# A five-stage attention kernel: GpSimd's root goes ahead of its gathers, the next x is normalised two slots sooner, and the next projection weights are loaded ahead of the spread

## What is computed

```python
xn = layernorm(x) * g + b
q, k, v = xn @ wq, keys @ wk, keys @ wv        # keys: xn itself in stages 2 and 3, else the context
p = exp(scale * (q @ k.T) + mask)
o = (p @ v) / p.sum(-1)
x = x + o @ wo + bo
if stage in (0, 2, 4):
    x = x + gelu(layernorm(x) @ w1 + b1) @ w2 + b2
```

## Time and profile before

| | |
|---|---|
| median of the runs shown | 5038.94 us |
| the profiled execution, its own time | 5035.45 us |
| its span, first to last instruction | 5033.6 us |
| around the span | 1.85 us |
| TensorE (PE) busy | 4666.1 us, 93% of the span |
| VectorE (DVE) busy | 3036.8 us, 60% |
| ScalarE (ACT) busy | 2308.4 us, 46% |
| GpSimd (POOL) busy | 1068.9 us, 21% |
| DMA, mean | 40 GB/s |
| bodies 0 to 41 | from 0 to about 3790 us, the tail behind it |

### The profile page before, as it was taken

One profiled execution on the slowest core, in us unless ns is written; L12 is line 12 of the kernel. 1 busy time (PEld: TensorE's weight loads), 2 busy tenths in 40 slices (PEclk: granted clock), 3 DMA queues, 4 the chain that ended last, 5 costly groups with the idle time before them and its releaser, 6 DMA issues.

```text
span 5033.6 us, 66240 instructions
## 1 busy us (share of the span) xinstructions
PE 4666.1 (93%) x24484; PEld 1880.0 (37%) x24484; DVE 3036.8 (60%) x7970; ACT 2308.4 (46%) x3011; POOL 1068.9 (21%) x991
## 2 busy tenths in 40 slices
PE   6999999989998999999988889999989999999999
PEld 2333333433332333343444433333333333333333
DVE  6777776556767777665565565555534455545554
ACT  4454554456664444434445454444443333333332
POOL 0111211111111211111111111211113333333333
PEclk9999999999999999999999999999999999999999
DMA  1111111121121111001211121111120000000000
GB/s 60 35 51 52 48 41 44 35 87 56 58 66 51 37 37 33 30 31 42 73 61 56 57 71 42 52 37 35 39 77 21 13 1 13 13 13 13 1 13 9
DMA packets 164465, 201.67 MB, mean 40 GB/s; under 512 B 36273, under 2 KB 119601, under 8 KB 162866
## 3 DMA queue, kind: packets, MB, share of 16 engines
q1 hardware_dynamic: 141106, 176.34, 10.5%
q0 software_dynamic: 23040, 21.10, 1.7%
HBM read 128.86 MB, written 68.42 MB: 39 GB/s over the span
## 4 chain that ended last, share of the span: by engine, by line
PE 61%; issue 19%; DVE 14%; ACT 4%; POOL 1%; DMA 1%; DVEq 0%; SPq 0%; POOLq 0%; ACTq 0%
PE psO L721 8%; PE small L650 8%; PE psT L696 6%; PE small L657 5%; PE psT L926 5%; PE psS L678 4%; PE psT L779 3%; DVE nmb L1171 3%; PE psT L650 2%; PE psT L886 2%; PE psO L941 2%; PE psT L896 2%; PE psT L941 2%; PE psT L702 2%; DVE xn L1148 2%
## 5 line engine op out<-in xcount | busy, mean ns | idle before, releaser
L991 ACT ACTIVATE probs<-psT 128x1024 f32<-128x1024 f32 (+3 forms) x1280 | 1159.7, 960 | 1211.2 <-PE psT L696 1042.0
L1171 DVE TENSOR_REDUCE nmb<-psS 128x1 bf16<-128x512 f32 x1024 | 649.8, 685 | 293.4 <-PE psS L678 292.8
L1168 DVE CUSTOM_DVE_ANT_0 out<-psS,pens_sb 128x512 f32<-128x512 f32 x1024 | 665.4, 685 | 250.4 <-issue 248.7
L696 PE MATMUL psT<-low 32*128 32x512 f32 (+3 forms) x5120 | 755.0, 608 | 29.4 <-ACT probs L991 26.5
L721 PE MATMUL psO<-probs,V 128*32 128x512 f32 (+3 forms) x5120 | 670.5, 597 | 20.6 <-DVE probs L1180 19.0
L678 PE MATMUL psS<-out 32*128 32x512 bf16 (+3 forms) x2560 | 595.6, 380 | 97.1 <-DVE nmb L1168 46.4
L1354 DVE TENSOR_REDUCE parts<-psS 128x2 bf16<-128x1024 f32 x256 | 314.9, 1230 | 531.4 <-PE psS L913 531.4
L1097 ACT ACTIVATE probs<-psT 128x1024 f32<-128x1024 f32 x256 | 262.0, 1023 | 524.9 <-PE psT L929 524.9
L678 PEld LDWEIGHTS psS<-out 32*128 32x128 bf16 x2560 | 148.6, 91 | 796.9 <-issue 444.0
L779 PE MATMUL psT<-out,W 128*128 128x512 f32 x768 | 382.9, 620 | 0.4
L1021 ACT ACTIVATE low<-small,vec 128x256 f32<-128x256 f32 (+1 forms) x464 | 261.9, 617 | 232.8 <-PE small L650 232.7
(11 more groups left out here) (178 smaller groups left out, 5942.4 us busy)
## 6 DMA issues: line engine op xcount, KB each, us to landing
o_mid<-out SPq DMA_DIRECT2D x160, 256.0 KB, 2.0
oN<-o_mid POOLq DMA_DIRECT2D x160, 128.0 KB, 3.5
oN<-r_mid SPq DMA_DIRECT2D x80, 256.0 KB
x_mid<-xe SPq DMA_DIRECT2D x40, 512.0 KB, 2.9
xw<-x_mid SPq DMA_DIRECT2D x36, 512.0 KB, 4.1
xe<-x_mid SPq DMA_DIRECT2D x36, 512.0 KB, 5.0
cT<-ctxT SPq DMA_DIRECT2D x20, 512.0 KB, 5.5
W<-wm SPq DMA_DIRECT2D x6, 1024.0 KB, 8.5
```

Of the source, the lines that this page charges most:

```text
L696: last = nc.tensor.matmul(psT[j][:, q0:S], Kf[rows_of(j), q, a, c, kt * P:(kt + 1) * P], Qf[rows_of(j), q, a, c, q0:S], start=True, stop=p ...
L991: nc.scalar.activation(probs[:, i % 2, two, q0:S], psT_all[:, two, q0:S], ACT.Exp, scale=float(DH) ** -0.5)\
L1168: nc.vector.tensor_tensor_reduce(junk[:, e, 0:n], psS[e][:, 0:n], penalty, 1.0, -3.0e38, ALU.add, ALU.max, at).then_inc(sem[f"s_read{e}"], 1)
L1171: nc.vector.tensor_reduce(at, psS[e][:, 0:n], AX, ALU.max).then_inc(sem[f"s_read{e}"], 1)
```

## The change

It makes three edits.

1. GpSimd does `rsqrt(nxt, 1)` ahead of `gather_outputs(prev)`.
2. The statistics of the next x stand in slots 0 and 1 instead of 2 and 3. Its normalisation stands in slot 3 (first half) and slot 4 (second half) instead of all in slot 5.
3. On SP the wait for v3 and the load of the next stage's Wqkv come ahead of `spread_recips` also where `prev` is in an MLP stage (bodies 8 and 24). The load of the context keeps its place and its wait.

```diff
-X_STATS, X_NORMALISE = (2, 3), (5, 5)
+X_STATS, X_NORMALISE = (0, 1), (3, 4)
...
                 late = prev is not None and prev.s in MLP
+                if new_stage:
+                    wait_taken(sp, place, "cur", "v3")
+                    sp.dma_start(Wqkv[:], wa[nxt.s, :, 0:N_QKV]).then_inc(qkv_in, 16)
                 if late:
                     spread_recips(prev)
-                if cur is not None and (new_keys or new_stage):
-                    wait_taken(sp, place, "cur", "v3")
-                if new_stage:
-                    sp.dma_start(Wqkv[:], wa[nxt.s, :, 0:N_QKV]).then_inc(qkv_in, 16)
                 if new_keys:
+                    if cur is not None:
+                        wait_taken(sp, place, "cur", "v3")
                     sp.dma_start(cT[:], keys).then_inc(sem["ctx_in"], 16)
                 if prev is not None and not late:
                     spread_recips(prev)
...
             def body(place, prev, cur, nxt):
+                if nxt is not None:
+                    rsqrt(nxt, 1)
                 if prev is not None:
                     gather_outputs(place, prev)
-                if nxt is not None:
-                    rsqrt(nxt, 1)
                 if prev is not None:
                     pool.wait_ge(sem["xe_in"], count("xe_in", prev, 16))
```

## The result

The changed kernel took 5009.2 us (median of five runs, 5001.9 to 5022.6) against 5038.9 before: the ratio is 0.9947, 95% interval 0.9934 to 0.9959. So it is faster by 0.53%, about 27 us, where 66 were forecast. The execution that was profiled is the fastest of the five, 5001.92 us; against the profiled one of before (5035.45) it gains 33.5 us. The comparison of the two traces is of these two executions, so it shows somewhat more than the medians do: the profiled execution has a mean clock of 0.985, the other four 0.980 to 0.982.

A forecast was written before the change was run, and what follows sets the result against it. TensorE bounds the kernel, busy 93%, with 73.3 us of x0 waits and 121 us lost to its clock. Terms 29 + 29 + 0 + 1 + 0 + 0 + 7 = 66 us give 4969.5, median 4973; range 4925 to 5016.

The forecast's parts named there:

- rival C: x0's wait replaced by a new one as VectorE's reordered list delays maxima in step 1 or 3; 5013 us, chance 0.22.
- Reading of before: TensorE waits 73.3 us at x0 for VectorE's normalisation in bodies 2 to 39, and its clock falls behind those waits.
- Masked bodies: Twelve masked MLP bodies (2 to 7, 18 to 23): 19.5 us of waits and 10.5 of clock, less one; gain 29 us.
- Stage 3: Bodies 27 to 32: waits 19.6 us and clock 13.8, less 4.5 for VectorE's later maxima of step 3; gain 29 us.
- Stage 4: Bodies 34 to 39: the finished unit's way ends last, so TensorE stands at y instead of x0; gain about 0.
- Stage 1 with 10, 17 and 33: Bodies 10 to 17 and 33: 9 us of waits and 6 of slow stretches go, as much comes back; 0, bounds -10 and +12.
- Wqkv: Bodies 8 and 24: q projection stops waiting for its weights, while the spread takes some back; gain 7 us, bounds 0 and 12.
- Rival D: VectorE's normalisation holds up GpSimd's issue of the gathers, costing 12 us in bodies 9, 25, 34 to 39; 4985 us, chance 0.08.
- A: The forecast itself: x0's wait goes and y caps stage 4; 4973 us, own bounds 4945 to 5005, chance 0.52.
- B: Nothing caps: all 73 us of waits go, 50 us of slow stretches are recovered, y follows; 4911 us, chance 0.10.
- E: Root still late because the statistics wait for xw in slot 0, so the order changes nothing; 5039 us, chance 0.04.
- F: Statistics in slots 0 and 1 delay m1 and v2, so TensorE stands in step 1 of every body; 5087 us, chance 0.04.

## Why the prediction was right and wrong

The sign and the range (4925 to 5016) held, the 66 us did not: 27 by the ratio, 34 in the traces. That the range held is owed to rival C, for whose sake it reached so far up, and not to the forecast's own bounds (4945 to 5005).

- **Reading of before**: x0's wait and the clock behind it, right as far as they went. All 38 waits went. But I put the lateness of xn down to the root and the slot. The run with the add first in the old order shows that the add's place alone was worth 1.23%, some 60 us, and 45.8 of the 73.3 us of waits.
- **Masked bodies**, 29 forecast, 33.6 measured. Right: in body 4 the add had begun before the second pair and was past half, and the pair took 1.68 us.
- **Stage 3**, 29 forecast, 7.6 measured, 6.0 of these in body 32. The step that failed is "two tiles each, between maxima", costed at 0.75 us in step 3 of VectorE. It measured 3.16 us. I had written that the add runs beside the normalisation in stages 3 and 4 and makes it 3.00 us, and then took the clear duration for the moved halves: I moved the root past the gathers and wrote that the bias add queues behind them, but never asked where in VectorE's list it would then fall. With the add out of the way stage 3 gained 31.2, so the rest of the term stood.
- **Stage 4**, 0 forecast, 9.5 us lost. That the way of the finished unit ends last was right, and "nothing in this way starts sooner" too. But the held pair made it start later: the reciprocals stand 8.6 us into each of bodies 34 to 39 and not 5.3, and y waits 20.1 us. With the add first the reciprocals stand at 6.0 and the stage is 1.6 us below before.
- **Stage 1 with 10, 17 and 33**, 0 forecast with bounds -10 and +12, 7.5 lost: 5.6 in body 17 and 2.9 in body 10, while 33 gained 2.8. In body 10 it was the hold (one tile of the second pair took 2.60 us; with the add first the body falls from 74.1 to 69.2). In body 17 the hold is one of two things. The limit took 3.17 us beside the add and TensorE waited 2.20 us behind it; the three us from 1546 have a clock of 0.63. With the add first this wait is gone, but a wait for maxima 4.7 us into the body is followed by six us at half clock, and the body is 97.0 us for 97.8 (92.2 in before). Body 17 of the changed kernel, then of the kernel with the add first (the wait, and the window behind it):

```profile
1540.60 3.17 DVE L1181 TENSOR_TENSOR probs<-probs,parts 128x1024 f32<-128x1024 f32 x1
1544.45 0.39 PE L679 MATMUL psS<-out 32*128 32x512 bf16 x1 [2.20 <-DVE nmb L1169]
```

```profile
1522.92 0.39 PE L679 MATMUL psS<-out 32*128 32x512 bf16 x1 [1.50 <-DVE nmb L1169]
...
1524.00:1530.00 6.00, 6.00 (x23) 2.12 (x22) 4.41 (x16) 0.00 (x0) 2.52 (x4) 0.50 0.39 91
```

  Body 17 of the changed kernel has such an early wait too, 1.36 us at 3.5 us into the body, and before has none over 0.6 there. That is the "stall of 1.4 us in step 1" of the prediction.

- **Wqkv**, 7 forecast: 8.9 in bodies 8 and 24 of the changed kernel, part of it the x0 waits; 6.6 (one trace) in the run with this edit alone. Right.
- **Rival C** came nearest in time (5013 to 5009) and said where: a new wait in the same place. It was right for stage 3 and wrong for the masked bodies, and its cause, VectorE's reordered list, is not what the runs show, but for the early wait in body 17.
- **Rival D** had the right pair of engines and the wrong way round. Beside the normalisation the gathers' issue took 2.50 to 2.64 us, where it takes 2.50 alone, so 0.14 us at most; it is VectorE that is held, by the add. The Trainium skill's page "SBUF — State Buffer" (Who interferes with whom) has both directions: whichever of the two issues first keeps the port pair for its whole instruction, and a VectorE instruction with two SBUF inputs contends with a GpSimd instruction that reads SBUF, as does one in a 2-port mode. The trace agrees with that for the limit, in both directions: 3.24 us for 1.22 in the rows of the run with both halves in slot 3; and in body 4 of before, where a limit has its start 0.17 us ahead of the adds of the MLP bias, the limit took its 1.22 and the first add 1.64 us for 0.72. That the loser is out for one instruction of the other fits body 27 of before (0.82 us a tile) and not the changed kernel: there one tile lasted 2.43 us beside adds of 0.7 us each. I used the half of the rule that speaks of descriptors and not the half that priced the change.
- **A** (4973) and **B** (4911) lie on either side of what the kernel gives with the add first (4945), 28 and 34 us away; **E** and **F** did not come, but F's mechanism is what the second edit does alone, with the root's wait in place of m1 and v2: 92 us slower.

## What to carry to other kernels

When an instruction is moved past others on one engine, follow what stood behind it: it now starts at another time, and may fall on another engine's work. In this kernel the long chain of adds did least harm where VectorE read PSUM or did other work that it doesn't hold; where such a chain can't be moved, cutting it in shorter instructions is worth a try: it let VectorE in, in most bodies. And price the edits of a change together: here two lose 37 and 92 us alone and gain together.

## What the runs showed of the hardware

- Beside four back-to-back adds of 128x256 f32 on GpSimd, one f32 `tensor_scalar` tile from SBUF to SBUF lasted 2.43 us (body 27) and 2.57 (body 35) of the changed kernel against 0.41 clear; in before, each of four tiles took 0.81 or 0.82 us beside the same four adds. A 128x1024 limit took 3.17 us (body 17 of the changed kernel) and 3.24 (body 4 with both halves in slot 3) against 1.22, and 3.26 beside one GpSimd multiply of 128x1024 (the scale in body 3 of the changed kernel). Row maxima, which read PSUM, were not slowed where it could be seen: in body 32 of the changed kernel three of 128x512 beside the adds took 0.69 us each, their usual time.
- Adds of 128 columns instead of 256 cost GpSimd 17% more time (234.1 us for 199.4 in the changed kernel), and VectorE's tiles took 524 ns instead of 777 in the mean.
- The clock fell to 0.68 over seven us behind a wait of 2.45 us in body 27, and read 1.00 over the whole of stage 3 in the run with the add first, where the waits for row maxima are 0.3 us at most. It doesn't fall behind every such wait: in before, a wait of 1.48 us was followed by seven us at 0.76 in body 4 and at 1.00 in body 3.
